# Eight images on one core: the first image's transfers issued from two queues, its scores in two buffers, and minima, layer-norm algebra, positional and residual sums off VectorE

## What is computed

```python
def tok(x):                       # 32x32 = 1024 tokens of 128
    xs = concatenate([x, *_shift4(x)], axis=-1)
    y = conv(xs, conv_w, strides=(16, 16)) + conv_b
    return (layernorm(y, eps=1e-3) * gamma + beta) @ dense_w + dense_b
def attn(x):                      # 8 heads of 64, causal
    q, k, v = split(x @ W_in + b_in)
    a = softmax(mask(q @ k.T * 64 ** -0.5))
    return (a @ v) @ W_out + b_out + x
def ffn(x):                       # 8 heads of 16
    x = x + depthwise_conv3(x, pos_w) + pos_b
    q, k, v = x @ qkv_w.T + qkv_b
    logits = q @ k.T * 128 ** -0.5
    keep the 16 largest logits of each row, softmax over them
    return (p @ v) @ wo_w.T + wo_b
h = concatenate([tok(x), txt])    # 1101 tokens, 9 tiles of 128 rows
h = h + attn(layernorm(h))
h = h + ffn(layernorm(h))
```

## Time and profile before

| | us |
|---|---|
| median of three runs (lowest to highest) | 4133.57 (4127.76 to 4135.05) |
| profiled execution, its own time | 4142.41 |
| its span | 4140.6 |

### The profile page before, as it was taken

One profiled execution on the slowest core, in us unless ns is written; L12 is line 12 of the kernel. 1 busy time (PEld: TensorE's weight loads), 2 busy tenths in 40 slices (PEclk: granted clock), 3 DMA queues, 4 the chain that ended last, 5 costly groups with the idle time before them and its releaser, 6 DMA issues.

```text
span 4140.6 us, 92874 instructions
## 1 busy us (share of the span) xinstructions
PE 3434.1 (83%) x34936; PEld 2239.0 (54%) x34936; DVE 3575.8 (86%) x5062; ACT 2268.4 (55%) x5793; POOL 1829.9 (44%) x2985
## 2 busy tenths in 40 slices
PE   4877788988988899988998899988988788975555
PEld 4645555555556555555555565555555455543333
DVE  0222599999999999999999999999999999999997
ACT  1655455655665566656665566655665556642222
POOL 2333444454444544454444544454444544442222
PEclk7999999999999999999999999999999999987777
DMA  5200300021100300021100310021000200010000
GB/s 78 52 5 3 88 20 3 3 53 33 25 3 9 79 20 13 8 52 30 20 13 8 79 23 10 4 53 33 15 5 2 60 15 2 2 41 18 13 1 6
DMA packets 233210, 103.54 MB, mean 25 GB/s; under 512 B 195441, under 2 KB 210242, under 8 KB 232770
## 3 DMA queue, kind: packets, MB, share of 16 engines
q1 hardware_dynamic: 228448, 95.64, 10.3%
q10 hardware_dynamic: 4322, 1.97, 0.4%
HBM read 78.86 MB, written 18.67 MB: 24 GB/s over the span
## 4 chain that ended last, share of the span: by engine, by line
DVE 46%; issue 24%; PE 16%; POOL 8%; SPq 3%; ACT 2%; ACTq 0%; DMA 0%; DVEq 0%; POOLq 0%
DVE A L1546 13%; DVE top L1551 10%; DVE M L1560 9%; DVE top L1539 8%; PE bank_ps L988 3%; DVE newmax L1492 3%; POOL PB L912 2%; PE bank_ps L1104 2%; POOL M L946 2%; PE score_ps L1076 2%; PE bank_ps L1167 2%; PE bank_ps L1173 2%; PE logit_ps L1145 1%; ACT PB L1302 1%; DVE negmax L1489 1%
## 5 line engine op out<-in xcount | busy, mean ns | idle before, releaser
L946 POOL TENSOR_SCALAR M<-M,to_mark 128x1101 bf16<-128x1101 bf16 x576 | 731.3, 1270 | 1209.8 <-DVE M L1560 1199.8
L1383 ACT ACTIVATE PT<-bank_ps 128x512 f32<-128x512 f32 x1296 | 755.7, 600 | 676.9 <-PE bank_ps L1173 673.0
L1539 DVE MAX8 top<-logit_ps 128x8 f32<-128x1101 f32 x576 | 749.4, 1301 | 93.9 <-PE logit_ps L1145 93.5
L1551 DVE MAX8 top<-A 128x8 f32<-128x1101 f32 x576 | 749.5, 1301 | 7.3 <-issue 0.2
L1546 DVE MATCH_REPLACE8 A<-top,logit_ps 128x1101 f32<-128x1101 f32 x576 | 746.6, 1296 | 0.9 <-issue 0.9
L1560 DVE MATCH_REPLACE8 M<-top,A 128x1101 bf16<-128x1101 f32 x576 | 744.1, 1292 | 1.2 <-issue 1.2
L1167 PE MATMUL bank_ps<-stack 128*128 128x512 bf16 (+5 forms) x1728 | 571.6, 345 | 131.4 <-POOL M L946 111.6
L1302 ACT ACTIVATE PB<-score_ps,negmax 128x512 f32<-128x512 f32 (+3 forms) x896 | 527.1, 595 | 197.9 <-DVE negmax L1489 131.7
L1321 ACT COPY PTc<-bank_ps 128x512 f32<-128x512 f32 (+2 forms) x800 | 424.7, 546 | 273.8 <-PE bank_ps L988 271.0
L1173 PE MATMUL bank_ps<-turn_m,M 128*128 128x128 bf16 (+1 forms) x5184 | 571.2, 226 | 0.0
L1076 PE MATMUL score_ps<-qk 64*128 64x512 f32 (+4 forms) x1920 | 446.1, 541 | 113.7 <-ACT PB L1302 111.3
(11 more groups left out here) (144 smaller groups left out, 4062.5 us busy)
## 6 DMA issues: line engine op xcount, KB each, us to landing
stack<-qk_parts SPq DMA_DIRECT2D x512, 72.0 KB, 2.7
X<-in_x SPq DMA_DIRECT2D x248, 60.8 KB
X<-in_x SPq DMA_DIRECT2D x248, 57.0 KB
qk_parts<-OT SPq DMA_DIRECT2D x16, 864.0 KB, 5.1
Wp<-in_L_attn_W_in SPq DMA_DIRECT2D x96, 64.0 KB, 2.0
out<-H SPq DMA_DIRECT2D x8, 512.0 KB
X<-in_x SPq DMA_DIRECT2D x248, 3.6 KB
stack<-in_L_tok_conv_w ACTq DMA_DIRECT2D x30, 64.0 KB
```

What stands on the lines that cost most here:

```text
L946: nc.gpsimd.tensor_scalar(M[:, n % M_SLOTS, :], M[:, n % M_SLOTS, :], to_mark[:, 0:1], to_mark[:, 1:2], ALU.mult, ALU.add).then_inc(marked, 1)
L1383: nc.scalar.activation(PT[0:rows, q % P_SLOTS, :], where[0:rows, :], ACT.Exp).then_inc(free(group), 1)
L1539: nc.vector.max(top[:, n % M_SLOTS, 0:8], logit_ps[:, 0:L]).then_inc(top8, 1)
L1551: nc.vector.max(top[:, n % M_SLOTS, 8:16], A[:, n % 2, :]).then_inc(top16, 1)
```

## The change

It has five parts.

1. **Front end.** The 30 fold transfers, all from ScalarE's queue before, are split: 15 from SP (ahead of its 18 weight loads) and 15 from ScalarE; the clearing memset of that buffer is cut in five so that each shift can start by itself; the four additions that fold the weight go from GpSimd to VectorE. A tile of patches is loaded in four steps r = 0 to 3 of 3 transfers; for image 0, ScalarE issues r = 1 and 3 and SP r = 0 and 2. Copies `copy_x` and `copy_y` of image 0 go from ScalarE to VectorE.
2. **Scores of image 0** alternate between `score_ps` and the first 1024 columns of `logit_ps` (`score_bufs(0)` is 2); from image 1 on there is one buffer as before.
3. **Off VectorE, all images.** The minimum is dropped: each piece keeps its own maximum, and GpSimd's gap step now forms the least of the pieces (two instructions more) and corrects all pieces, the last too. AGGREGATE, variance and newton go: GpSimd computes mean and variance from the six statistics (6 small instructions) and newton (5). The two positional additions go to GpSimd, ScalarE preparing both scaled taps (two instructions more, into `qk`). The residuals of `res` and `outp` are added on TensorE by one more f32 matmul with `ident` for each of the 18 tiles, and ScalarE copies the result out.
4. **Image 0's k side** is copied out and split on VectorE (part1, part2, part3) while GpSimd splits q, and the K half of the first `stack` quarter is issued by ScalarE.
5. **The plan**: costs and some due times change with it (tokenizer of image 1 later, transfers due nearer to their use), and so the order on every engine.

```diff
+def score_bufs(c):
+    return 2 if c == 0 else 1
...
-        t0 = c0 - 30 * STEP
+        front = "DVE" if c == 0 else "ACT"
+        t0 = c0 - (12 if c == 1 else 30) * STEP
-            add("SP", 5.0, due - 60, ("load_x", c, i), *prior, lag=3.0)
+            for r in range(4):
+                add("ACT" if c == 0 and r % 2 else "SP", 2.0, due - (60 if c == 0 else 25), ("load_x", c, i, r), *prior, lag=3.0)
...
-        add("DVE", 0.2, due, ("var_t", c), *[("stat_t", c, i) for i in range(NPT)])
+        add("POOL", 1.2, due, ("var_t", c), *[("stat_t", c, i) for i in range(NPT)])
...
-                    *([("exp_part", *FILL[m - 1])] if m else []), ("keep_p", c, p, 0, i // 4),
+                    *([("exp_part", *FILL[m - score_bufs(c)])] if m >= score_bufs(c) else []),
...
-        add("DVE", 1.4, due + 14, ("pos1", c), ("pos0", c))
-        add("DVE", 1.4, due + 14, ("pos2", c), ("pos1", c))
+        add("POOL", 2.4, due + 14, ("pos1", c), ("pos0", c))
+        add("POOL", 2.4, due + 14, ("pos2", c), ("pos1", c))
...
+            if (c, s) == (0, 1):
+                add("DVE", 1.4, due + 17, ("part1", c), *[("keep_f", c, s, g) for g in range(3)])
...
@@ gpsimd
+                    m_even, s_even, m_odd, s_odd = (st[:, k, 0:n, q] for q in (1, 2, 4, 5))
+                    settle_ln(nc.gpsimd.tensor_tensor(v, m_even, m_odd, ALU.subtract))
+                    settle_ln(nc.gpsimd.tensor_tensor(v, v, v, ALU.mult))
...
+                    for hh in range(2):
+                        of_pieces = [negmax[:, s, j, hh:hh + 1] for j in range(J + 1)]
+                        if J == 1:
+                            last = nc.gpsimd.tensor_scalar(least[:, s, hh:hh + 1], of_pieces[0], of_pieces[1], None, ALU.min)
...
+                elif event == "pos1":
+                    pool.wait_ge(pos_first, c + 1)
+                    nc.gpsimd.tensor_tensor(xpT[:, 1:L], xpT[:, 1:L], qk[:, 2, 0:L - 1], ALU.add).then_inc(pos_v, 1)
@@ tensor
-                        last = nc.tensor.matmul(where[:, q0:q0 + 128], OT[:, q, 128 * t:128 * t + 128], Wo1[:, q, :],
-                                                start=(q == 0), stop=(q == NP - 1))
+                        nc.tensor.matmul(where[:, q0:q0 + 128], OT[:, q, 128 * t:128 * t + 128], Wo1[:, q, :],
+                                         start=(q == 0), stop=False)
+                    last = nc.tensor.matmul(where[:, q0:q0 + 128], ident[:, :], H[:, t, :], start=False, stop=True)
@@ vector
+            dve.wait_ge(fold_loaded[0], 16 * 6)
+            dve.wait_ge(fold_loaded[1], 16 * 6)
+            nc.vector.tensor_tensor(Wf[0:KU], fold[0:KU, 0], fold[0:KU, 1], ALU.add).then_inc(folded, 1)
...
-                    settle(nc.vector.bn_stats(st[:, k, i, :], src))
-                    nc.vector.bn_aggr(mv[:, k, i, :], st[:, k, i, :]).then_inc(ln_v, 1)
+                    nc.vector.bn_stats(st[:, k, i, :], src).then_inc(measured[k], 1)
...
-                        nc.vector.reduce_max(newmax[:, :], score_v[:, :, 0:z - a], AX.X, negate=True
-                                             ).then_inc(max_v, 1)
...
-                        nc.vector.tensor_tensor(negmax[:, s, j, :], newmax[:, :], negmax[:, s, j - 1, :], ALU.min
-                                                ).then_inc(rowmax, 1)
+                    nc.vector.reduce_max(negmax[:, s, j, :], score_v[:, :, 0:z - a], AX.X, negate=True
+                                         ).then_inc(rowmax, 1)
```

More of the change, by code:

```diff
@@ L232, in arrange, with splitter @@
         return order
+def splitter(c, s):
+    return ("part3", c) if (c, s) == (0, 1) else ("split3", c, s)
 def make_plan():
@@ L405, in make_plan @@
             add("POOL", 2.5, due + 17, ("split3", c, s), ("split2", c, s))
-        add("SP", 0.2, due + 18, ("save", c), *[("split3", c, s) for s in range(2)],
+        add("SP", 0.2, due + 18, ("save", c), *[splitter(c, s) for s in range(2)],
             *([("stack", c - 2, 3)] if c >= 2 else []), lag=6.0)
```

374 lines of the change are left out of this document (229 added, 145 removed).

## The result

| | before | changed |
|---|---|---|
| median of six runs (lowest to highest), us | 4132.14 (4127.76 to 4140.34) | 4115.08 (4112.73 to 4124.79) |
| ratio, 95% interval | | 0.9962 (0.9947 to 0.9977) |
| span of the profiled execution | 4140.6 | 4111.3 |

The account below looks back on a forecast made before the run. VectorE was taken to set the pace in the periods, chains between engines in the start. Start -52, six periods -39, first period -2 and tail +1 gave -92 us, from 4133.57 to 4042; range 3968 to 4095.

Parts of the forecast that it names:

- the sum of the periods: Periods after the start: VectorE's relief less the wait given back, -6.5 us for each of six (-39); first period -2.
- Front end: Start up to the first scores: three terms, -23 us in all, first scores at 102 instead of 125.
- the second: Front end, image 0's patches issued from two queues: -15.7 us from first transposes to last statistic (between -5 and -20).
- The third term: Front end, chain from last statistic to first scores: longer GpSimd algebra +2.6, shorter wait for `X` -3, together -0.4 us.
- Attention of image 0: Start, first scores to about 396: two score buffers let TensorE go ahead by a fill, -25 us (-12 to -40).
- Image 0's change: Start, image 0's change to sparse work: save ahead of patches and sides split on two engines, -4 us (+4 to -14).
- VectorE's relief: Periods: statistics, minimum, positional sum, variance and newton, and residuals leave VectorE, 21.0 us per image.
- The wait at the change of image: Periods: VectorE waits 14 us for the next image's first logits by TensorE's order; 14.5 of 21 us given back.
- B: Rival: only the start gains; TensorE or longer layer-norm and gap chains hold the period at 466; 4081 us, chance 0.2.
- D: Rival: slower, the wait at the change of image exceeds what VectorE saves; 4143 us or more, chance 0.05.

Follow-up runs that it names:

- e11: e4_start with all of image 0's patches issued by SP's queue again, fold transfers still on two queues; 4049.6 us, ratio 0.9793.
- e6: e4_start with one score buffer for image 0 instead of two; 4096.75 us, ratio 0.9912.
- e1: Changed kernel with layer-norm tiles in the old multiply-then-add form, order untouched; 4064.11 us, ratio 0.9829.
- e2: Changed kernel with the steps at an image's end due 20 us earlier in the plan; 4074.17 us, ratio 0.9854.
- e3: Changed kernel with both the old form of the layer-norm tiles and the steps of an image's end due 20 us earlier; 4021.45 us, ratio 0.973.
- e5: Kernel before with GpSimd's layer-norm tiles in the subtract-then-multiply form, nothing else moved; 4186.96 us, ratio 1.0124.
- e8: Changed kernel with the positional sums back on VectorE; 4110.11 us, ratio 0.9944.
- e4_start: Changed kernel with layer-norm algebra, minima, positional and residual sums on VectorE again; 4042.49 us, ratio 0.9777.

## Why the prediction was wrong, step by step

The step that failed is the sum of the periods: it priced GpSimd's layer-norm tile at its old 0.45 us, where the new form takes 0.79, and it let no wait grow but the one at the change of image. The points in the order of the prediction:

- **Front end**: -23 forecast, -10.1 measured (first scores at 115.1). The transposes began at 39.0, forecast 37. The term that failed is the second: from there to the last statistic (83.14) 44.1 us, where I had 34 and the earlier trace rows 49.7. Two queues took off 5.6 us and not 15.7. I counted issuing time and 6 us for the last piece. Two things were left out, and no run separates them. Tiles 1 to 7 share two buffers: ScalarE's queue ended an issue at 54.95 and began the next at 57.89, which I read as a wait for one. And the transfers slow each other, which I had only as the reason for the end at -5: between the first transposes and the last statistic the transfer engines were busy 0.80 at 79 GB/s, where they were busy 0.33 at 62 before. e11 shows the two queues' worth directly: 7.3 us at the first scores. The Trainium skill's rule (DMA: Bandwidth & Descriptors, "Issuing engines are not separate DMA queues") would have had it near zero, my sum 16; the run lies between. The third term, +0.3 for the -0.4 forecast, was right by luck: the chain of 32.0 us holds 5.8 us for the slower form of 17 tiles, which I had not counted.
- **Attention of image 0**: -25 forecast, -62 measured, outside my end of -40. I let 17.3 us of waits go and a part of the rest. Nearly all of TensorE's idle time went (44.0 us before, 3.1 now), and its busy time fell by 20.9 us with a granted clock of 1.00 instead of 0.93, where I had taken it as fixed. e6 shows that the second buffer alone does it.
- **Image 0's change**: -4 forecast, +3.4 measured (61.5 for 58.1), within its bounds; e1 shows that the form was part of it.
- **VectorE's relief**: 21.0 us per image forecast, 17.7 measured; right in kind and nearly in size.
- **The wait at the change of image**: 14.5 us given back, forecast from the rows of the order; measured, over the last twelfths of images 2 to 4, 18.9 us idle where 2.2 were, so 16.7. The mechanism and nearly the size were right, TensorE's row being the longer way as I had said. Due times 20 us earlier took 7.2 us of it away per image and 41 to 43 us of the whole (e2, e3).
- **What the sum of the periods lacked**: two terms. One is the form of the layer-norm tile, which I had taken at its old 0.45 us without a row for the new one: 51 us of the whole (e1, e5), some 9 in the start and 40 in the periods. The other is the waits outside the last twelfth, 10.7 us more per image (27.4 more idle in all, 16.7 of them at the change), where I had let none grow. Per image of 2 to 4 the sum said -6.5 and the rows say +9.7; of the 16.2 us between, 3.3 are the relief that fell short, 2.2 the larger wait and 10.7 these waits. The form makes up 6.4 of the 16.2 (e1); what makes the rest is open. For the whole: with the form priced, the sum would have been 4042 + 51 = 4093, inside the range. The start did 25 us better than the sum with its part of the form in it, which gives 4068. Of the other 47 us, the relief that fell short is some 23, and the rest is waits.
- **The rivals**: B (periods unchanged, 4081) was the nearest. Of its two reasons TensorE's load was not it, since e1, with the same matmuls, is 51 us faster; longer layer-norm chains were part of it, by a form that B did not name. D had the right sign for the periods: they lost 40 us, and only the start kept the whole below the kernel before.

## What to carry to other kernels

Price an operation moved to another engine in the exact form that it takes there; here subtract-then-multiply in place of multiply-then-add decided 51 us. Where a plan orders the work from costs, changing the costs is a change of its own: read the new order at each hand-over, and give the moved chain an earlier due time before judging the move. An engine relieved of 18 us in a period of 466 gives back only what its feeders can deliver: measure the relief with the form mended and the order as far as it can be (here 23 to 26 us of a possible 115), and against the part that stands without it (here the second buffer, 54 us by itself).

## What the runs showed of the hardware

GpSimd's TENSOR_SCALAR with two per-row operands on 128x128 f32 takes 451 to 453 ns on average as multiply then add in the kernel before (448 to 482 in the others with that form) and 794 to 815 ns as subtract then multiply in the four with this one (the changed one, e2, e5, e8), with the other engines idle or busy (the first ones at 87.0 us, when VectorE did nothing). The same instruction with minimum as its operation on 128x1 takes 277 ns, and 364 with two minima. TensorE's busy time for nearly the same matmuls of one attention was 226.7 us where its waits made up a sixth of the stretch (granted clock 0.93, a mean between the levels of 1.2 and 2.4 GHz) and 206.1 us where it hardly waited (1.00, the upper level). Issuing image 0's patches from two queues instead of one doubled the busy share of the transfer engines for that stretch (0.73 in e4_start, 0.37 in e11) and brought the first scores 7.3 us forward.
